# One barrier at each layer border, and layer-norm statistics one tile behind the additions in the projecting blocks of an eight-layer network

## What is computed

```
x = x + L0_attn_a(layernorm(x))     # 16-head attention with gates on the scores
x = x + L0_ffn(layernorm(x))        # ternary weights
x = x + L0_attn_b(layernorm(x))     # gated delta rule, 6 heads
x = x + L0_ffn(layernorm(x))
x = x + L1_attn_a(layernorm(x))     # 16-head attention
x = x + L1_ffn(layernorm(x))        # 8 experts, top 2, low-rank
x = x + L1_attn_b(layernorm(x))     # latent attention, causal
x = x + L1_ffn(layernorm(x))
```

## Time and profile before

| | us |
|---|---|
| median of 3 runs (lowest, highest) | 1435.81 (1435.34, 1439.43) |
| span of the profiled execution, first to last instruction | 1435.6 |
| busy: PE, DVE, ACT, POOL | 1349.0, 895.4, 694.1, 278.4 |
| mean granted TensorE clock | 0.984 |
| the four projecting blocks start at | 236.6, 531.5, 837.4, 1275.3 |
| the seven layer borders, first barrier lets go | 253.6, 325.7, 552.8, 625.9, 854.4, 1001.5, 1290.8 |
| the same, second barrier lets go | 254.5, 326.2, 554.3, 626.4, 855.3, 1002.1, 1291.6 |

### The profile page before, as it was taken

The page is one execution under the profiler, slowest core; times in us unless marked ns, Lnnn a source line. Parts: engine busy times, 40 slices in busy tenths (PEclk is TensorE's granted clock), DMA queues, the critical chain, the costliest instruction groups (busy, mean ns, idle before and its releaser), DMA issues. The chain is left out here.

```text
span 1435.6 us, 32894 instructions
## 1 busy us (share of the span) xinstructions
PE 1349.0 (94%) x13699; PEld 738.4 (51%) x13707; DVE 895.4 (62%) x2147; ACT 694.1 (48%) x1037; POOL 278.4 (19%) x343
## 2 busy tenths in 40 slices
PE   7999998999679988999999989999899999989999
PEld 3355555474345774563555554436355555555436
DVE  3899994666486456749999826433655555535431
ACT  5487776646483325535777752111444444442110
POOL 4322513001230000043000000110533433210110
PEclk9999999999879999999999999999999999999999
DMA  3323300100300000022222030000300000000000
GB/s 87 70 38 65 65 14 1 34 1 2 118 0 4 17 1 16 0 45 42 43 39 36 3 117 0 1 0 7 64 13 17 15 13 14 9 1 1 1 0 29
DMA packets 33957, 37.47 MB, mean 26 GB/s; under 512 B 9153, under 2 KB 24626, under 8 KB 33810
## 3 DMA queue, kind: packets, MB, share of 16 engines
q1 hardware_dynamic: 33810, 35.39, 11.2%
HBM read 18.43 MB, written 1.07 MB: 14 GB/s over the span
## 5 line engine op out<-in xcount | busy, mean ns | idle before, releaser
L616 DVE TENSOR_REDUCE row_max_pieces<-psum 128x1 f32<-128x512 f32 (+3 forms) x672 | 406.9, 647 | 112.4 <-PE psum L510 109.7
L717 ACT ACTIVATE probs<-psum 128x1024 f32<-128x1024 f32 (+7 forms) x384 | 343.7, 900 | 212.6 <-PE psum L510 212.2
L564 PE MATMUL psum<-probs,v_ones 128*32 128x256 f32 (+1 forms) x2688 | 238.8, 376 | 9.0 <-POOL probs L499 4.6
L510 PE MATMUL psum<-q_all,k_head 97*32 97x512 f32 (+3 forms) x1536 | 190.7, 487 | 0.0
L510 PE MATMUL psum<-k_stack,q_stack 96*32 96x512 bf16 x2048 | 158.8, 379 | 3.5 <-DMA k_stack<-arena 1.3
L510 PE MATMUL psum<-q_stack,k_stack 97*32 97x512 bf16 x2048 | 157.8, 379 | 0.0
L564 PEld LDWEIGHTS psum<-probs,v_ones 128*32 128x32 f32 x2688 | 88.0, 109 | 85.1 <-POOL probs L499 21.6
L510 PE MATMUL psum<-k_head_bf,q_all_bf 80*32 80x512 bf16 (+3 forms) x768 | 93.0, 328 | 2.3 <-ACT k_head_bf L2487 1.1
L510 PEld LDWEIGHTS psum<-q_all,k_head 97*32 97x32 f32 x1536 | 78.8, 109 | 29.5 <-issue 3.9
L510 PEld LDWEIGHTS psum<-k_stack,q_stack 96*32 96x32 bf16 x2048 | 56.5, 95 | 72.1 <-DVE row_max_pieces L616 20.4
L510 PEld LDWEIGHTS psum<-q_stack,k_stack 97*32 97x32 bf16 x2048 | 58.3, 96 | 49.4 <-ACT probs L717 3.7
(11 more groups left out here) (368 smaller groups left out, 2085.6 us busy)
## 6 DMA issues: line engine op xcount, KB each, us to landing
q_stack<-arena SPq DMA_DIRECT2D x32, 96.0 KB, 2.7
k_stack<-arena SPq DMA_DIRECT2D x32, 96.0 KB, 2.6
arena<-gd_g_sums SPq DMA_DIRECT2D x6, 512.0 KB, 6.1
q_stack<-arena SPq DMA_DIRECT2D x32, 64.0 KB, 2.3
k_stack<-arena SPq DMA_DIRECT2D x32, 64.0 KB, 2.3
x_tokens<-in_x SPq DMA_DIRECT2D x4, 256.0 KB, 3.6
k_stack<-arena SPq DMA_DIRECT2D x32, 32.0 KB, 2.3
q_stack<-arena SPq DMA_DIRECT2D x32, 32.0 KB, 2.0
```

Of the source, the lines that this page charges most:

```text
L510: last = pe.matmul(o[j:j + 32], by[:, j:j + 32], rows, **flags)
L564: last = pe.matmul(psum[32 * g:32 * g + VW, PVB, a - g * D:D], V[:, c, h, :], pr[:, n % PB, a:(g + 1) * D], start=(c == 0), stop=(c == (2 ...
L616: last = dve.reduce_max(mx[:, h % 2, qt, i:i + 1], o[:, 0:plain], AX.X)
L717: act.activation(pr[:, n % PB, q_from(c):], psum[:, 2 * (n % 2):2 * (n % 2) + 2, :].rearrange("p a n -> p (a n)")[:, q_from(c):], ACT.Exp, ...
```

## The change

`layer_done` no longer clears and no longer has a barrier. It puts the semaphores of the layer on a list, and the next layer clears them on GpSimd with `clear_retired`: at the start of its own block in `ternary_ffn` and `routed_ffn`, at the start of its projecting block in the attention layers and the gated delta layer. They are thus still taken while the next layer takes its own.

In `project_out`, DVE runs `dve_behind` instead of `dve`: after the addition of tile t it takes the statistics of tile t - 1, after an odd tile the mean and variance of pair (t - 3) / 2 ahead of that, after an even tile from 4 on the reciprocal and shift of pair t / 2 - 2. After tile 7 stand pair 2's and pair 3's. The odd tiles of pairs 0 to 2 are normed by GpSimd (`by_pool`), that of pair 3 by DVE, which counts on a semaphore of its own (`xn_last`). `pe_behind` and ACT's program are as before.

```diff
--- before.py
+++ after.py
@@ -41,7 +41,7 @@
         self.shift = self.sb("minus_mean_rstd", [P, NT], F32)
         self.eps = self.sb("norm_eps", [P, 1], F32)
         self.arena = self.sb("arena", [P, ARENA], F32)
-        self.next_sems = []
+        self.next_sems, self.retired = [], []
         self.stored = nc.alloc_semaphore("stored")
         self.psum = self.ps("psum", [P, 8, HALF], F32)
 
@@ -65,9 +65,13 @@
 
     def layer_done(self):
 
-        self.nc.clear_and_free_semaphores(self.sems)
+        self.retired += self.sems
         self.sems, self.next_sems = self.next_sems, []
-        self.nc.all_engine_barrier()
+
+    def clear_retired(self):
+
+        self.nc.clear_and_free_semaphores(self.retired)
+        self.retired = []
 
 
 class Norm:
@@ -79,36 +83,66 @@
 
     PAIRS, BEHIND = NT // 2, 3
 
-    def __init__(self, core, tag, scope, room=None, awaited=2):
-        self.core, sem, self.awaited = core, lambda n: core.sem(f"{tag}_next_{n}"), awaited
+    def __init__(self, core, tag, scope, room=None, awaited=2, by_pool=0):
+        self.core, sem, self.awaited, self.by_pool = core, lambda n: core.sem(f"{tag}_next_{n}"), awaited, by_pool
         self.xn = core.sb("xn", [P, NT, D], F32, scope) if room is None else room
         self.summed, self.mv_done, self.std_done, self.rstd_done, self.shift_done = (
             sem(n) for n in ("summed", "mean_var", "std", "rstd", "shift"))
-        self.xn_even, self.xn_odd, self.turned, self.taken = (
-            sem(n) for n in ("xn_even", "xn_odd", "transposed", "taken"))
-
-    def dve(self, dve, t):
-        core = self.core
-        dve.bn_stats(core.stats[:, t, :], core.X[:, t, :]).then_inc(self.summed, 1)
-        if t % 2:
-            dve.wait_ge(self.summed, t + 1)
-            for i in (t - 1, t):
-                dve.bn_aggr(core.mv[:, i, :], core.stats[:, i, :]).then_inc(self.mv_done, 1)
-        elif t:
-            self.dve_pair(dve, t // 2 - 1)
-        if t == NT - 1:
-            self.dve_pair(dve, self.PAIRS - 1)
-
-    def dve_pair(self, dve, p):
+        self.xn_even, self.xn_odd, self.xn_last, self.turned, self.taken = (
+            sem(n) for n in ("xn_even", "xn_odd", "xn_last", "transposed", "taken"))
+
+    def stats(self, dve, t):
+        dve.bn_stats(self.core.stats[:, t, :], self.core.X[:, t, :]).then_inc(self.summed, 1)
+
+    def moments(self, dve, p):
+        dve.wait_ge(self.summed, 2 * p + 2)
+        for i in (2 * p, 2 * p + 1):
+            dve.bn_aggr(self.core.mv[:, i, :], self.core.stats[:, i, :]).then_inc(self.mv_done, 1)
+
+    def inverse(self, dve, p):
         core, two = self.core, slice(2 * p, 2 * p + 2)
         dve.wait_ge(self.std_done, p + 1)
         dve.reciprocal(core.rstd[:, two], core.std[:, two]).then_inc(self.rstd_done, 1)
         dve.wait_ge(self.rstd_done, p + 1)
         dve.scalar_tensor_tensor(core.shift[:, 2 * p:2 * p + 1], core.mv[:, 2 * p:2 * p + 1, 0], -1.0,
                                  core.rstd[:, 2 * p:2 * p + 1], ALU.mult, ALU.mult).then_inc(self.shift_done, 1)
-        t = 2 * p + 1
-        dve.tensor_scalar(self.xn[:, t, :], core.X[:, t, :], core.mv[:, t, 0:1], core.rstd[:, t:t + 1],
-                          ALU.subtract, ALU.mult).then_inc(self.xn_odd, 1)
+        if p >= self.by_pool:
+            self.odd(dve, p)
+
+    def odd(self, eng, p):
+        core, t = self.core, 2 * p + 1
+        eng.tensor_scalar(self.xn[:, t, :], core.X[:, t, :], core.mv[:, t, 0:1], core.rstd[:, t:t + 1],
+                          ALU.subtract, ALU.mult).then_inc(self.xn_last if p == self.PAIRS - 1 else self.xn_odd, 1)
+
+    def dve(self, dve, t):
+        self.stats(dve, t)
+        if t % 2:
+            self.moments(dve, t // 2)
+        elif t:
+            self.inverse(dve, t // 2 - 1)
+        if t == NT - 1:
+            self.inverse(dve, self.PAIRS - 1)
+
+    def dve_behind(self, dve, t, added):
+
+        if t >= 3 and t % 2:
+            self.moments(dve, (t - 3) // 2)
+        if t:
+            dve.wait_ge(added, t)
+            self.stats(dve, t - 1)
+        if t >= 4 and t % 2 == 0:
+            self.inverse(dve, t // 2 - 2)
+        if t == NT - 1:
+            self.inverse(dve, self.PAIRS - 2)
+            dve.wait_ge(added, NT)
+            self.stats(dve, NT - 1)
+            self.moments(dve, self.PAIRS - 1)
+            self.inverse(dve, self.PAIRS - 1)
+
+    def pool(self, pool):
+        for p in range(self.by_pool):
+            pool.wait_ge(self.rstd_done, p + 1)
+            self.odd(pool, p)
 
     def act(self, act):
         core = self.core
@@ -131,7 +165,10 @@
 
     def pe(self, pe, p):
         pe.wait_ge(self.xn_even, p + 1)
-        pe.wait_ge(self.xn_odd, p + 1)
+        if p == self.PAIRS - 1:
+            pe.wait_ge(self.xn_last, 1)
+        else:
+            pe.wait_ge(self.xn_odd, p + 1)
         for f in range(KT):
             for i in range(2):
                 last = pe.transpose(self.core.psum[:, p, f * D + i * P:f * D + (i + 1) * P],
@@ -314,6 +351,10 @@
             @block.sync
             def _(sp):
                 loads(sp)
+
+            @block.gpsimd
+            def _(pool):
+                core.clear_retired()
 
             @block.tensor
             def _(pe):
@@ -990,12 +1031,17 @@
     turned, kept, ready, added = (core.sem(f"{tag}_{n}") for n in ("o_turned", "o_features", "proj", "added"))
     with ExitStack() as tmp:
         OT = core.sb("attended_features", [P, tiles, S], F32, tmp) if OT is None else OT
-        norm = Norm(core, tag, tmp, xn, 1)
+        norm = Norm(core, tag, tmp, xn, 1, by_pool=Norm.PAIRS - 1)
         with nc.Block() as block:
             if next_loads:
                 @block.sync
                 def _(sp):
                     next_loads(sp)
+
+            @block.gpsimd
+            def _(pool):
+                core.clear_retired()
+                norm.pool(pool)
 
             @block.tensor
             def _(pe):
@@ -1031,8 +1077,7 @@
                 for t in range(NT):
                     dve.wait_ge(ready, t + 1)
                     dve.tensor_tensor(X[:, t, :], psum[:, 4 + t % 4, 0:D], X[:, t, :], ALU.add).then_inc(added, 1)
-                    dve.wait_ge(added, t + 1)
-                    norm.dve(dve, t)
+                    norm.dve_behind(dve, t, added)
 
 
 
```

## The result

The changed kernel takes **1466.8 us**, median of 4 runs (1460.8 to 1475.8), beside 1436.0 (1435.3 to 1439.4) for the kernel before on the same chip: 1.0207 times as long, with an interval of 1.0175 to 1.0239. The sign was forecast, the size was not: 1447.3 was predicted, and the range ended at 1457. The profiled execution took 1462.6 us, of which the span is 1460.8, so 25.2 us over the span of before.

The account below looks back on a forecast made before the run. DVE was taken to pace blocks aa, ac and la, PE block gd. 1435.8 us, less 5.7 for the borders, plus 17.2 lost in the projecting blocks (3 x 4.0 + 5.2), gave 1447.3 us; range 1443 to 1457.

Parts of the forecast that it names:

- The sum of the order: Four projecting blocks: reciprocals moved behind later additions lose 4.0 us each in aa, ac, la and 5.2 in gd, together 17.2.
- the step from transposes to the next addition: Projecting blocks: from a pair's transposes to the addition of the next tile, 2.15 us in gd and 1.72 in aa.
- The term for the end of the chain: Projecting block, from tile 7's addition to the last transposes: 3.6 us instead of 2.58, 1.0 us more.
- The borders: Seven layer borders: removing the second barrier and the clears there gains 5.7 us, all on the path.
- The clears: GpSimd at the next layer's start: 17 range clears instead of 8, costed at nothing; without cover under 3 us once.
- I take 0.8, since it is the same kind at half the width: GpSimd's odd tile in the projecting blocks: 0.8 us, with 0.78 (half of L282) below and 0.73 (L931) beside it.
- rival B: GpSimd takes 1.57 us for the odd tile; pairs 0 to 2 wait longer, 9 us more, 1456 us; chance 0.05.
- the clock as a rival: The clock falls in the thinner projecting blocks, 2 to 3.5 us each, 1449 to 1459 us; chance 0.30.
- A: Rival: the clock falls in one to four projecting blocks, 2 to 3.5 us each, 1449 to 1459 us; chance 0.30.
- C: Rival: DVE's relief pays for the longer end of the projecting blocks, leaving the barriers' 5.7 us gain, 1430 us; chance 0.06.
- D: Rival: lateness in the projecting blocks is only half the forecast, 8.6 us, giving 1438.7 us; chance 0.09.
- The sentence on the DRAIN rule: DVE in the projecting blocks: by the rule three steps come 0.2 us later each, some 2 us more in all.

Follow-up runs that it names:

- e3: The changed kernel with the odd tiles back on DVE, statistics still one tile behind: 1449.5 us, ratio 1.0085 to the kernel before.
- e6: The changed kernel with PE's transposes 5 tiles behind instead of 3 and the odd tiles back on DVE: 1431.2 us, ratio 0.9976 to the kernel before.
- e7: The kernel before with the changed borders and PE's transposes 5 tiles behind instead of 3, DVE's order and odd tiles as before: 1432.3 us, ratio 0.9960.
- e2: The kernel before with only the projecting blocks changed, second barrier and clears at the border as before: 1476.1 us, ratio 1.0261.
- e8: The changed kernel with two filling matmuls, results unused, ahead of the transposes of pairs 0, 1 and 2: 1448.6 us, ratio 1.0086 to the kernel before.
- e9: The changed kernel with only the subtraction in GpSimd's odd tiles, the multiplication left out: 1454.8 us, one run.
- e5: The changed kernel with PE's transposes in the projecting blocks 5 tiles behind instead of 3: 1435.1 us, ratio 0.9987 to the kernel before.
- e1: The kernel before with only the borders changed, the projecting blocks as before: 1431.2 us, ratio 0.9960.

## Why the prediction was right and wrong

**The mechanism was right.** The transposes of pair 0 and 1 had to wait for a reciprocal that had moved behind a tile which PE makes later, and DVE then waited for PE. With the odd tiles on DVE the steps came where they were put, after the first addition in la: reciprocal of pair 0 at 4.13 us (predicted 4.11), its transposes at 5.16 (5.14), those of pair 1 at 9.28 (9.44), the addition of tile 7 at 10.84 (11.16), the last transposes at 14.53 (14.76). The sum of the order, 17.2 us, measured 16.4. The largest error in it is the step from transposes to the next addition, which comes twice in a block: it was taken as 2.15 us in gd and 1.72 in aa, and is 1.99 and 1.56 in e3 (gd and la). The prediction counted it from PEld's weight load at 543.33, while its other steps end at PE's transposes, which start here in the kernel before:

```profile
543.55 0.60 PE L137 MATMUL psum<-identity,t_inverse_transposed 128*128 128x128 f32 x4
```

The term for the end of the chain, 1.0 us, measured 1.0 (e6 beside e7 in gd).

**The borders** gave 5.0 to 5.3 us instead of 5.7. "Nothing else shows between the release and the first matmul, so I take it that the second barrier hides no other work" fails at border 5, where a transfer of weights is late next. The clears cost nothing that shows, as said: they were over before each first odd tile was due.

**First step that failed: "I take 0.8, since it is the same kind at half the width".** The odd tile takes 1.22 us. Half of L282 was the low bound, the addition L931 stood beside it, and I took the two for agreement; but L282's width was not all that set its time, nor was L931 the same kind. From the reciprocal to the transposes of pair 0 it took 1.65 us (244.42 to 246.07) instead of 1.05. Of the 0.6 us more, 0.45 is the operation (1.25 against 0.8), and the rest is the handovers, 0.11 and 0.14 us where 0.10 in all was counted. It comes at each of the three pairs: PE's waits are 2.36, 2.33 and 2.61 against 1.74, 1.74 and 2.03 in e3. The transposes of pair 0 started at 246.07, close to the 246.3 forecast, but that is luck: the first addition came at 240.29 instead of 241.19, with a clock of 1.00 from 237 to 241 where it had been 0.57. From it they came 5.78 us later instead of 5.14 and those of pair 1 at 10.47 instead of 9.44. Over the four blocks it is 5.2 us, where the sum had nothing for it; rival B had asked for 9 at 1.57 us.

The Trainium skill (GPSIMD Engine Reference, 4.1 Engine selection) calls one-input operations on GpSimd roughly line-rate. The trace speaks against it for this operation: the same instruction over 128x256 elements takes 1.22 us on GpSimd and 0.41 on DVE.

**Second step that failed: the clock as a rival at 0.30, outside the forecast.** It fell in every block of both profiles of the changed kernel, and of e2. Its price was right in the mean: 2 to 3.5 us a block were given, and 9.6 us over four blocks is 2.4 each. Single blocks lie on both sides of that: against e8 they lost 1.9, 3.9, 1.8 and 2.0 us in the first profile and 0.9, 4.1, 3.3 and 4.0 in the second. "3.8 to 7 us at half speed were seen" leaves out two long stretches of the kernel before, with a clock of 0.51 from 366.5 to 379.5 us and 0.50 from 414.5 to 430.5. The sum was off too: four falls at 2 to 3.5 us end at 1455 to 1461, not at 1459. The chance of 0.30 was too low, and the prediction had reason to see that: it computed idle times of 1.7, 1.6 and 2.2 us in a row and held a single thin stretch at the border of gd against them, where one wait is followed by work (PE busy 3.50 of the next 4 us, clock 1.00).

How likely a fall is does not follow from the length of the waits alone. With 1.74, 1.74 and 2.03 us (e3) the clock fell in two blocks of four, with 2.04, 2.02 and 2.31 (e9) in one of four, and with 2.36, 2.33 and 2.61 in four of four, three times over. With a single long wait, 1.76 to 1.78 us ahead of pair 2, it fell in aa and la of e5 but not in ac, and at 1.72 to 1.73 in no block of e7. So that GpSimd's longer waits made falls likelier is plausible, and not shown.

A and B were priced as if only one of them could be true, so the sum of both, 1447.3 + 9.6 + 5.2 = 1462, lay outside the range. The profile bears it out: -5.3 + 16.4 + 5.2 + 9.6 = 25.9 us against the 25.2 by which the spans differ. Only the -5.3 of e1 and the 31.2 of the blocks are independent here, since the other three terms are shares of the 31.2. The median of 1466.8 is 4 us above the profiled execution, and the longer executions had the lower clock: over the four runs the mean granted clock of the whole execution is 0.980, 0.976, 0.970 and 0.969, and the times, in the same order, 1460.8, 1462.6, 1471.0 and 1475.8 us.

**The rivals C and D** fell at the point named for C: pair 0's transposes in aa came 5.78 us after the first addition, where C needed 4.0. D needed half of the 17.2 us, and the order alone took 16.4. Even with PE's waits mostly out of the way, both halves of DVE's relief together made a block longer (12.41 us in ac in e5 against 12.02).

The sentence on the DRAIN rule can be closed as well. The trace shows an addition at 252.47, recorded with 0.43 us, and the next instruction, which awaits nothing from it, 0.34 us later at 252.81, against 0.46 from an addition to its own statistics. So what is not awaited does start ahead of its predecessor's recorded end. The Trainium skill (VectorE: DVE Perf Modes, The DRAIN you can't avoid) puts it behind the emptied pipe, but adds in the same place that a next operation that is not held starts earlier, which the prediction left out. The trace agrees with that second part. The 2 us that the rule would have added did not come.

## What to carry to other kernels

When a producer's order is shifted by a step, shift its consumer's order by as much, or the shift comes back as a wait at each step and, through buffers or an in-order queue, as a wait of the producer too: here one number on PE turned a loss of 2.1% into a tie, in which the borders' gain of 5 us is spent. Ask of each half of a relief what it is worth by itself: the odd tiles on GpSimd paid with the old order and lost with the new one. Price an operation that is new on an engine from a row of the same operation on that engine, or let the range take in everything between the bounds. Where a change makes PE stand several times in succession, add the fall of its clock to the forecast itself, and try filling matmuls in the wait if the wait can't be removed.

## What the runs showed of the hardware

GpSimd takes 1.22 us for subtract and multiply with a value per partition over 128x256 f32, 0.93 for the subtraction alone and 0.73 for adding two tiles of that size: three quarters of the time are there with one operation, and this addition with a second input tile takes less than this subtraction with a value per partition.

The granted clock differs from one execution to the next of one program, and with it the time, by 15 us over four runs of the changed kernel. PE's waits in two profiled executions were the same to 0.05 us, and yet the clock was 0.85 in la in one and 0.68 in the other. So the fall needs the idle stretches, as e8 shows by filling them, but whether and where in the block it comes, and for how long, the waits alone don't say. What sets that stays open.
